# A graph-and-attention kernel on one core: other nodes for unused edge slots, earlier edge loads, two groups joined inside the layers, W_fx fetched early

## The reference, cut to what matters

```python
xn = _layernorm(x)
# graph part, 4 heads of 64:
feats = einsum('nd,hdo->hno', xn, Ws) + bs
score = a_s[:, src] + a_d[:, dst] + aw_e * elem + ab
w     = exp(-relu(score / 20))
out   = segment_sum(w * feats[dst], src) / segment_sum(w, src)
# mix part: 4 layers of
x = x + linear_attention(layernorm(x))       # softmax keys over the nodes
x = x + gelu(layernorm(x) @ W1 + b1) @ W2 + b2
# then, with X = x + graph + mix, the last part on layernorm(X):
slice_weights = softmax((X_n @ W_x @ W_slice + ...) / temp)
slice_token   = slice_weights^T @ (X_n @ W_fx + b_fx), small attention over 64 tokens
out           = X + (slice_weights @ out_slice) @ W_out + b_out
```

## Time and profile before

| | |
|---|---|
| median of 3 runs | 3572.68 us (3567.56 to 3574.93) |
| the profiled execution's own time | 3563.9 us |
| its span, first to last instruction | 3562.2 us |
| PE busy | 3266.9 us (92%) |
| DVE busy | 2342.1 us (66%) |
| POOL busy | 1977.8 us (56%) |
| mean granted TensorE clock | 0.968 |

### The profile page before, as it was taken

One profiled execution on the slowest core, in us unless ns is written; L12 is line 12 of the kernel. 1 busy time (PEld: TensorE's weight loads), 2 busy tenths in 40 slices (PEclk: granted clock), 3 DMA queues, 4 the chain that ended last, 5 costly groups with the idle time before them and its releaser, 6 DMA issues.

```text
span 3562.2 us, 43962 instructions
## 1 busy us (share of the span) xinstructions
PE 3266.9 (92%) x13948; PEld 2317.0 (65%) x13948; DVE 2342.1 (66%) x6105; ACT 1185.3 (33%) x2124; POOL 1977.8 (56%) x1745
## 2 busy tenths in 40 slices
PE   5788799999989999989989999898999999789979
PEld 3566566666756776666767666676676666555556
DVE  5887789885444444453468787776776676569941
ACT  2343233333333333333324444333434343322210
POOL 2211007777777777777737777774777777500000
PEclk9899899999999999999999999999999999899989
DMA  3332112222322222232245555554555557922234
GB/s 100 96 96 86 49 44 46 47 46 39 75 52 43 48 48 49 43 88 38 43 114 146 145 145 148 140 157 129 161 151 165 151 162 130 106 60 75 78 109 152
DMA packets 226436, 338.52 MB, mean 95 GB/s; under 512 B 52502, under 2 KB 180009, under 8 KB 225956
## 3 DMA queue, kind: packets, MB, share of 16 engines
q0 software_dynamic: 67840, 119.33, 17.9%
q1 hardware_dynamic: 120452, 161.93, 14.1%
q10 hardware_dynamic: 37920, 54.45, 4.9%
HBM read 247.40 MB, written 87.29 MB: 94 GB/s over the span
## 4 chain that ended last, share of the span: by engine, by line
PE 58%; POOL 16%; DVE 14%; issue 6%; DMA 4%; ACT 2%; DVEq 0%; SPq 0%; ACTq 0%
POOL arena L769 16%; PE bank_v L1707 13%; PE bank_a L1692 13%; PE bank_a L1609 4%; PE bank_e L1749 3%; PE bank_v L1637 3%; PE bank_v L1597 3%; PE bank_a L1538 3%; PE bank_v L1768 3%; PE bank_v L1680 3%; PE bank_v L1858 3%; PE bank_v L1780 2%; DMA arena<-gather_table,arena 2%; DMA arena<-edge_weight_parts 1%; PE bank_a L1588 1%
## 5 line engine op out<-in xcount | busy, mean ns | idle before, releaser
L800 POOL DMA_INDIRECT edge_records<-acc x800 | 964.6, 1206 | 512.5 <-issue 512.5
L769 POOL DMA_INDIRECT arena<-gather_table,arena x880 | 938.8, 1067 | 378.3 <-issue 258.6
L1707 PE MATMUL bank_v<-W_sb,gT 128*125 128x256 f32 x3200 | 743.5, 384 | 1.5 <-issue 1.5
L1692 PE MATMUL bank_a<-hT,W_sb 128*128 128x500 f32 (+1 forms) x1664 | 710.4, 575 | 12.3 <-issue 7.5
L1707 PEld LDWEIGHTS bank_v<-W_sb,gT 128*125 128x125 f32 x3200 | 589.5, 189 | 106.5 <-issue 24.5
L1692 PEld LDWEIGHTS bank_a<-hT,W_sb 128*128 128x128 f32 x1664 | 316.8, 193 | 318.6 <-issue 296.4
L1749 PE MATMUL bank_e<-arena 128*125 128x260 f32 x1760 | 457.4, 405 | 0.0
L826 ACT ACTIVATE gT<-bank_a,cols 128x500 f32<-128x500 f32 (+1 forms) x416 | 271.8, 661 | 371.3 <-PE bank_a L1692 365.2
L1749 PEld LDWEIGHTS bank_e<-arena 128*125 128x125 f32 x1760 | 323.3, 194 | 46.0
L826 ACT ACTIVATE hT<-bank_a,cols 128x500 f32<-128x500 f32 (+1 forms) x208 | 144.8, 747 | 485.7 <-PE bank_a L1538 485.7
L1150 DVE TENSOR_TENSOR arena<-arena 128x1024 f32<-128x1024 f32 x220 | 268.0, 1218 | 0.0
(11 more groups left out here) (285 smaller groups left out, 4332.7 us busy)
## 6 DMA issues: line engine op xcount, KB each, us to landing
residual<-xs SPq DMA_DIRECT2D x60, 500.0 KB
xs<-residual SPq DMA_DIRECT2D x60, 500.0 KB
arena<-edge_rows ACTq DMA_DIRECT2D x220, 125.0 KB
queries<-qT_out SPq DMA_DIRECT2D x48, 500.0 KB, 3.1
qT_in<-queries ACTq DMA_DIRECT2D x39, 500.0 KB
arena<-gather_table,arena POOLq DMA_INDIRECT x880
edge_records<-acc POOLq DMA_INDIRECT x800
slice_weights<-arena SPq DMA_DIRECT2D x12, 1000.0 KB, 5.0
```

What stands on the lines that cost most here:

```text
L769: e.indirect_dma_start(g_of(j)[:, i, :], None, table_d, bass.IndirectOffsetOnAxis(ap=node[:, TE * j + i:TE * j + i + 1].bitcast(I32), axis ...
L800: e.indirect_dma_start(rec_d, bass.IndirectOffsetOnAxis(ap=pos_i[:, f:f + 1], axis=0), r3[:, f, :], None).then_inc(d_rec, 16)
L1692: o = e.matmul(b[:, 0:n], W[:, k, f * P:(f + 1) * P], hv[:, k, 0:n], start=k == 0, stop=k == KC - 1)
L1707: o = e.matmul(b[0:R, i % 2 * D:(i % 2 + 1) * D], gv[:, f, i * R:(i + 1) * R], W2_sb[:, f * D:(f + 1) * D], start=False, stop=f == FB - 1 ...
```

## The change

Five edits:

- Unused slots: `blank` gets, in place of node 0, node j + 42 p for slot j of partition p (42 is (6250 - 880) // 127). This is one more POOL instruction.
- `src`, `dst`, `edge_weight` are fetched by SP behind the small bias loads of the start; to make that safe the sort's arrays, the bias arrays and `oh` lie elsewhere in `acc`.
- The sort's preparation is four steps at planned distances of 7.0 in place of three at 3.0 and a fourth at 12.0 (old step 2 is split, so all later steps have a number one higher).
- `join 0` is due at `added - 14`, `join 1` at `added - 3.5`; the blocks end at `added - 32`. SP's loads of residual rows for the joins move from `join s` to the `slice_logits` in front of it.
- W_fx, W_out and b_fx are fetched by SP at `total END` and no longer at `tokens`.

```diff
-    COUNT_STEP = 4 + NT // 2 + 3
+    FIRST_COUNT = 5
+    COUNT_STEP = FIRST_COUNT + NT // 2 + 3
...
-        at += 3.0 if k < 3 else 12.0 if at < mixed else 8.0 if k < COUNT_STEP else 4.5 if k < first_part else 7.0
+        at += 7.0 if k < FIRST_COUNT - 1 else 12.0 if at < mixed else 8.0 if k < COUNT_STEP else 4.5 if k < first_part else 7.0
...
-        inside = edges_at + 50.0 <= at <= added - 20.0 and sum(b <= i for b in between) % 2 == 1
+        inside = edges_at + 50.0 <= at <= added - 32.0 and sum(b <= i for b in between) % 2 == 1
...
-    beside.append((added - 6.0, ("join", 0)))
+    beside.append((added - 14.0, ("join", 0)))
+    beside.append((added - 3.5, ("join", 1)))
...
-        if s + 1 < NGR:
+        if 2 <= s + 1 < NGR:
             order.append(("join", s + 1))
...
+            for to, of in ((src_i, src), (dst_i, dst), (ew, edge_weight)):
+                e.dma_start(to, of.rearrange("(p n) -> p n", p=ER)).then_inc(d_edges, 16)
...
                 elif stage == "sort" and at[0] == 0:
-                    ev = lambda a: a.rearrange("(p n) -> p n", p=ER)
-                    e.wait_ge(slice_bias_set, 1)
-                    e.dma_start(src_i, ev(src)).then_inc(d_edges, 16)
-                    e.dma_start(dst_i, ev(dst)).then_inc(d_edges, 16)
-                    e.dma_start(ew, ev(edge_weight)).then_inc(d_edges, 16)
                     e.wait_ge(blank_set, 1)
...
-                elif stage == "join" and 1 <= at[0] < NGR - 1:
-                    s, = at
-                    e.wait_ge(*x_stored(DEPTH, s + 1))
-                    load_x(DEPTH + 1, s + 1, x_d[DEPTH % 2])
+                    if s == END:
+                        e.wait_ge(a_done, a_end("up", LAST, END, FB - 1))
+                        load_rows(d_wfx, W1_sb[:, 0:KC * SL], W_fx, KC)
+                        e.wait_ge(v_done, down_end(LAST, END))
+                        load_rows(d_wout, W2_sb[:, 0:PAIRS * D], W_out, PAIRS)
+                        e.dma_start(bfx, b_fx.partition_broadcast(P)).then_inc(d_bfx, 16)
+                elif stage == "slice_logits" and at[0] + 2 < NGR:
+                    s, = at
+                    e.wait_ge(*x_stored(DEPTH, s + 2))
+                    load_x(DEPTH + 1, s + 2, x_d[DEPTH % 2])
...
                 elif stage == "tokens":
-                    e.wait_ge(a_done, a_end("up", LAST, NGR - 1, FB - 1))
-                    load_rows(d_wfx, W1_sb[:, 0:KC * SL], W_fx, KC)
-                    e.wait_ge(v_done, down_end(LAST, NGR - 1))
-                    load_rows(d_wout, W2_sb[:, 0:PAIRS * D], W_out, PAIRS)
-                    e.dma_start(bfx, b_fx.partition_broadcast(P)).then_inc(d_bfx, 16)
                     e.wait_ge(wbd_zero, 1)
...
                     step(e.memset(blank, 0.0))
-                    e.memset(blank.rearrange("p (n k) -> p n k", k=3)[:, :, 1], -1.0).then_inc(blank_set, 1)
+                    b3 = blank.rearrange("p (n k) -> p n k", k=3)
+                    e.iota(b3[:, :, 0].bitcast(I32), [[1, SLOTS]], base=0, channel_multiplier=(N - SLOTS) // (P - 1))
+                    e.memset(b3[:, :, 1], -1.0).then_inc(blank_set, 1)
```

More of the change, by code:

```diff
@@ L374, in build_program @@
         NFLAT = 2 * KB + KC
-        bflat = acc[:, 10240:10240 + NFLAT]
+        bflat = acc[:, 11520:11520 + NFLAT]
         in_flat = ((bo, 0, KB), (b2, KB, KB), (b_out, 2 * KB, KC))
-        bparts = [acc[:, 10304 + 32 * i:10304 + 32 * i + NFLAT // 2].bitcast(BF16) for i in range(3)]
+        bparts = [acc[:, 11552 + 32 * i:11552 + 32 * i + NFLAT // 2].bitcast(BF16) for i in range(3)]
         bhi = acc[0:3, 7168:7168 + BO // 2].bitcast(BF16)
@@ L380, in build_program @@
         assert BO % 2 == 0 and 8960 + BO <= 10240
-        ab_sb = acc[0:3, NBIAS:NBIAS + HG]
-        bsl_sb = acc[0:3, NBIAS + 4:NBIAS + 4 + G]
+        ab_sb = acc[0:3, 3400:3400 + HG]
+        bsl_sb = acc[0:3, 3404:3404 + G]
         tmpw = acc[:, 4096:4096 + HG * DG].rearrange("p (h o) -> p h o", h=HG)
@@ L400, in carve @@
             return acc[0:rows, SA - n:SA]
+        oh = carve(EC)
         src_i, dst_i = carve(EC).bitcast(I32), carve(EC).bitcast(I32)
         ew = carve(EC)
-        srcf, bucket, rank, offs, oh, cum, pair = (carve(EC) for _ in range(7))
+        assert BO <= EC and SA <= 3400
+        srcf, bucket, rank, offs, cum, pair = (carve(EC) for _ in range(6))
         recs = carve(3 * EC)
@@ L409, in build_program @@
         thr = carve(TJ, TP)
-        assert SA <= 12480 and NT * HG <= ACC - 12500 and 3 * SLOTS <= 8000
+        assert SA <= 11520 and NT * HG <= ACC - 12500 and 3 * SLOTS <= 8000
         r3 = recs.rearrange("p (n k) -> p n k", k=3)
@@ L1075, in sort_step @@
                     step(e.scalar_tensor_tensor(row, bucket, -float(R), srcf, ALU.mult, ALU.add))
[L1076 to L1081, removed]
+                elif k in (2, 3):
+                    cmp, sign, bound = ((ALU.is_lt, -1.0, 0.0), (ALU.is_ge, 1.0, float(R)))[k - 2]
+                    step(e.tensor_scalar(oh, row, bound, sign, cmp, ALU.mult))
+                    step(e.tensor_tensor(bucket, bucket, oh, ALU.add))
+                    step(e.scalar_tensor_tensor(row, oh, -float(R), row, ALU.mult, ALU.add))
+                    if k == 2:
+                        e.tensor_copy(r3[:, :, 0].bitcast(I32), dst_i)
+                        return
                     e.tensor_copy(r3[:, :, 2], ew)
@@ L1084, in sort_step @@
                     step(e.memset(offs, 0.0))
-                elif k == 3:
+                elif k == 4:
                     step(e.tensor_scalar(pos_i, bucket, 1.0, None, ALU.mult))
@@ L1090, in sort_step @@
                     step(e.tensor_scalar(weight, odd_i, float(SHIFT - 1), 1.0, ALU.mult, ALU.add))
-                elif 4 <= k < 4 + NPAIR:
-                    b = k - 4
+                elif FIRST_COUNT <= k < FIRST_COUNT + NPAIR:
+                    b = k - FIRST_COUNT
                     step(e.scalar_tensor_tensor(oh, pair, float(b), weight, ALU.is_equal, ALU.mult))
@@ L1097, in sort_step @@
                     step(e.tensor_tensor(rank, rank, oh, ALU.add))
-                elif k == 4 + NPAIR:
+                elif k == FIRST_COUNT + NPAIR:
                     ci = low[:, 0:NPAIR]
```

## The result

The changed kernel took 3550.89 us (median of 4 runs, 3542.55 to 3554.23), the kernel before 3571.39 us beside it (4 runs, 3567.56 to 3574.93): a ratio of 0.9942, 95% interval 0.9923 to 0.9962, faster by 20.5 us. A second comparison on another chip gave 0.9934 (0.991 to 0.9957). The forecast of 3540 was 11 us too low; direction and range held, and so did the likeliest case's own range, 3525 to 3554. The profiled execution is the fastest of the four: its own time is 3542.55 us, its span 3540.8, against a span of 3562.2 before.

A forecast was written before the change was run, and what follows sets the result against it. POOL was taken to set the pace of the edge phase. The terms -26.9 - 25 + 9.9 + 12.2 + 3.3 - 6.5 = -33.0 took 3572.7 to 3539.7, so 3540 us, range 3510 to 3563.

The forecast's parts named there:

- the likeliest case: The forecast itself, the sum of all terms giving 3540 us: 60% chance, own range 3525 to 3554 us.
- Unused slots, -26.9: Second section of edge blocks: 464 gathers at POOL's 1.370 us, without the slow DMA stretch from 3000 to 3112.5; -26.9 us.
- The blocks' end, +12.2: End of the layers: layer work behind the edge blocks grows from 21.3 to 33.5 us; +12.2 us.
- The start, -25 + 9.9: Start: DVE's 19.9 us stall goes and counting steps move, -25 us; the plan starts POOL's edge work later, +9.9 us.
- I take half: Stretch before the layers: two counting steps moved out of it save 10 us of DVE time, of which half was counted.
- POOL runs without a break from the first scatter: Edge phase: POOL works unbroken from the first scatter at 533.96, so its start shifts with the plan, +9.9 us.
- Joins, +3.3: Last pass: DVE waits in `join 1` for residual rows, so `slice_sums 0` starts later; +3.3 us, bounds +6 and -10.5.
- W_fx, -6.5: At W_fx: prefetching removes the waits for W_fx and b_fx, DVE starts near 3423.2; -6.5 us.
- That the early hole closes only in part: Rival, 12%: the stall at the start closes only in part, -12 for -25, giving 3553 us.
- That the slots stay slow: Rival, 8%: slowness belongs to the table's place, not one row; without the 26.9 gain, 3567 us.
- PE's clock in the second section: Rival, 5%: in the second section of edge blocks PE waits more often, its clock falls, giving 3600 us.
- That POOL's pace leaves PE control: Rival, 15%, with join 1 getting its rows in time as alternative: 3526 us, 3518 without the plan's +22.1, 3504 with both.

The follow-up runs named there:

- same_row: `best` with the unused slots of one gather all naming one node, but another node for each gather: 3509.93 us, ratio 0.9834.
- node0: The changed kernel without the added iota, so unused slots name node 0 again: 3706.66 us, ratio 1.0022 to the kernel before on its chip.
- best: `old_spacing` with the edge blocks planned to 20 us before the layers' end and `join 0` due at 13.5: 3511.47 us, ratio 0.9835.
- group 1: First set of follow-up runs, the parts alone, on a chip where the kernel before takes 3694.64 us.
- slots_only: The kernel before with only the new node numbers in the unused slots: 3675.05 us, ratio 0.9937.
- early_only: The kernel before with only the edge arrays fetched behind the small loads: 3676.88 us, ratio 0.9945.
- best_count: `best` with the changed kernel's 7 us spacing of the sort's first steps, edge records due as in `best`: 3527.91 us, ratio 0.9882.
- old_spacing: The changed kernel with the sort's first five steps as close as before, bringing later sort steps, records and blocks forward: 3665.49 us, ratio 0.9911.
- os_oldjoins: `old_spacing` with the joins as in the kernel before: 3524.01 us, ratio 0.9866.

## Why the prediction was right, and where it was off

**Unused slots, -26.9: right, as to time.** The 464 gathers took 26.1 us less and the ring waits of the earlier trace rows are gone. The forecast was that they then run at POOL's pace of 1.370 us; they run at 636.4 / 464 = 1.372. What I gave as its reason, "spread over 128 different rows", was more than it takes. Many reads of one row within a gather cost little (`same_row`); slow is the same row read again by gather after gather, all through the last 17.5 blocks (`node0`, and the kernel before). No run named a fixed node other than 0. By the Trainium skill (DMA: Bandwidth & Descriptors, Latency and other measured facts), which has copies at half rate when partitions lie megabytes apart by powers of two, the new pitch of some KiB should not slow the packets. The trace agrees: 0.162 us.

**What the jam cost behind the last gather: not priced.** In the kernel before, the last edge sums came 24 us after the last gather (3136 against 3112), in the changed kernel 15. Without a jam and with the blocks' end at -20 (`best`) the way from the last gather to the logits is 40.4 us; the kernel before had 47.8. That is another 7.4 us, and the new node numbers alone account for 4.8 of it: on the chip of group 1 it is 43.5 us in `slots_only` and 48.3 in `early_only`.

**The blocks' end, +12.2: right, a little less.** It is 49.5 to 51.5 us with -32 and 40.3 to 40.4 with -20, that is +9 to +11. By way of `best` the table's +3.7 is a gain of 7.4 and a price of 11.1: the change both won and spent there.

**The start, -25 + 9.9: the step that failed.** The sum took "-25 in all" for the stall and "I take half" of the 10 us of moved counting steps. The stall did go: the first conversion starts at 62.87 without a DMA wait, and PE is 28 us ahead at 120 and 22 at 400. But from 400 to 560 it loses 15 us, and 7 are left at 560 (14 again for a while near 660, then 7 from 780 to 1600). `best_count` shows that the spacing alone does this, 10.8 to 14.7 us, not half of 10, and `early_only` and `best` show that the early fetch without it keeps 21 to 27 us until 1800. The step priced the wrong thing. The moved counting steps cost nothing that is left by 400, where `best_count` is 0.3 us behind. What costs is that all later sort steps move too, and three of them now stand inside the queries' norm and make PE wait, where `best` has one: 10.9 us in place of 3.2, and the rest of the 15 by the lower clock behind the waits. A cost counted in busy time of DVE could not show this; a step's place in the list decides it.

**How the start reaches the end.** I had "POOL runs without a break from the first scatter", so that its start would set its end. It has breaks, and in two of them it waits for PE's buffers (18.62 and 35.30 us in the timeline after, 27.8 and 36.6 before). Through these PE's lead sets the start of each section. The first section starts at 1871.05 after and at 1871.33 before: a lead of some 7 us cancels against a plan that is 9.9 us later. POOL sets only what lies within a section. So of the two terms the +9.9 was near the truth, and the -25 should have been about -7. The plan's part can be read off too: with the same spacing of the sort as `best_count`, but a later plan and an earlier end of the blocks, the changed kernel starts its second section 8.0 us later, 13.0 by its second profile.

**Joins, +3.3: right in mechanism, small in size.** DVE waits 13.63 us in `join 1` (forecast some 14), PE waits behind two logits tiles, 11.11 us, and the sums of group 0 start 37.0 us after the first logits, in place of 31.4: +5.6. The ring of three banks did not help as much as I had it do; why it is 5.6 and not 3.3 stays open.

**W_fx, -6.5: right.** PE's lead grows by 6.8 us at this place, from 14.8 to 21.6. Both waits of the earlier trace rows are gone:

```profile
3406.71 1.50 PE L1808 MATMUL bank_v<-W_sb,gT 128*128 128x128 f32 x12
3407.46 0.27 DVE L1494 SCALAR_TENSOR_TENSOR gT<-W_sb,Wqkv,bank_v 64x64 f32<-64x64 f32 x1 [0.52 <-PE bank_v L1808]
```

**The rivals.** That the early hole closes only in part was to give 3553, and 3551 came. Its number was right by another mechanism: the hole closed, and the lead was given back 300 us later. That the slots stay slow is out by `slots_only`, `node0` and `same_row`. PE's clock in the second section did not fall on average (0.98). It does dip in the edge phase, and behind waits far shorter than the 9.9 us of the jam: in the kernel before PE waits 2.46 us until 2176.7, and from 2177.8 to 2181.1 its granted clock is 0.50, the lower level of 1.2 GHz. That POOL's pace leaves PE control was half true: not within a section, but at its start.

**The number.** It held by some luck. The start came 17 us worse than forecast, and 8.5 us of that were hidden by the stretch behind the last gather, where a gain of 5 to 7 us had no term at all.

## What to carry to other kernels

A gain at the start is worth what is left of it at the next place where two engines meet. Follow the lead of one engine past each such place before adding it to a sum, and look for the same change's own edits between. A plan's due time is a discrete choice: half a microsecond moved `join 0` past `total 11` and was worth 9 to 12 us, and 11 us less room moved two blocks into the section where POOL sets the time. Price a moved step by what waits behind the place where it lands, not by its length. Slots that do no work still do transfers: give them addresses that vary from one gather to the next.

## What the runs showed of the hardware

**One row read again and again.** Packets of the gathers' queue: 0.16 to 0.17 us for rows of many nodes, 0.208 when the 128 rows of a gather are one but change from gather to gather, 0.515 and 0.543 when all gathers name node 0. Why repetition over time hurts more than repetition at once is open.

**DVE lengthens POOL's gathers.** The gathers in the edge phase have no single length. Timeline on DVE and POOL of the changed kernel:

```profile
2300.71 1.22 DVE L1158 TENSOR_TENSOR arena<-arena 128x1024 f32<-128x1024 f32 x1
...
2301.21 1.53 POOL L772 DMA_INDIRECT arena<-gather_table,arena  x1 [0.31 <-issue]
...
2301.85 0.35 DVE L1168 TENSOR_SCALAR arena<-arena,iota_part 125x512 bf16<-125x512 bf16 x1
...
2302.11 0.67 DVE L1162 TENSOR_TENSOR arena<-iota_row,arena 128x500 f32<-128x500 f32 x1
...
2304.30 0.95 POOL L772 DMA_INDIRECT arena<-gather_table,arena  x1 [0.30 <-issue]
...
2305.55 0.94 POOL L772 DMA_INDIRECT arena<-gather_table,arena  x1 [0.30 <-issue]
```

What counts is what DVE runs when a gather starts. Over the gathers after 1860, those that start with DVE idle take 0.945 us (278 of them). Those that start beside L1158, which weighs the fetched rows, take 1.39 us on average (211), up to 2.0 (the first gather shown, 1.53 us, is one of them); beside L1162 1.21 us (57). L1168 lengthens them hardly (0.956, 20 of them), and L1412, which reads PSUM, not at all (0.946, 128). The Trainium skill (SBUF — State Buffer, SBUF: two separate sides) says that DVE and GpSimd share one pair of SBUF ports, and that whichever starts first holds it for its whole instruction: DVE in its two-port modes, or with two SBUF inputs, then only against a GpSimd operation that reads SBUF. The trace agrees for two inputs, as L1158 and L1162 have them; a gather here reads its node numbers from SBUF. For the two-port modes no run here shows it. As POOL sets the pace of each section, L1158 and L1162 are a part of it: at 0.945 for the mean of 1.066, 464 gathers would be 56 us shorter, an estimate from these rows that nothing here tested.

**Chips differ where POOL sets the pace.** On the chip of group 1 the kernel before takes 3.4% longer. Until 1800 us the same kernels run alike (`old_spacing` is there at the lead that `os_oldjoins` has on the other chip). Then POOL waits for ring buffers from time to time, 59.8 us in 33 waits in `old_spacing`'s second section, where the changed kernel's profile on the first chip has none. The view calls them "remote", as it finds no instruction that ended them; each stands at the first gather of a block, on the semaphore of PE's sums:

```profile
POOL arena L772 <- issue: 125.3, 411, 0.3
POOL arena L772 <- remote: 59.8, 33, 3.2
POOL arena L772 <- PE bank_e L1757: 46.8, 12, 39.0
```

Its packets take 0.171 us there, as on the other chips. What makes the ring come free later stays open.
